# Two groups of four heads in one PSUM bank: one copy, sum broadcast, reciprocal, product and output projection for both

## The reference

```python
xn = _ln(x, ln1_w, ln1_b)
q, k, v = ((xn @ w + b).reshape(B, L, 16, 8) for w, b in ((q_w, q_b), (k_w, k_b), (v_w, v_b)))
scores = jnp.einsum('bqhd,bkhd->bhqk', q, k) * 8 ** (-0.5)
scores = jnp.where(causal, scores, -jnp.inf)
attn = jax.nn.softmax(scores, axis=-1)
attn_out = jnp.einsum('bhqk,bkhd->bqhd', attn, v).reshape(B, L, 128) @ o_w + o_b
...
x = x + alpha * attn_out + (1.0 - alpha) * ssm_out
```

## Time and profile before

| | |
|---|---|
| median of three runs | 1694.33 us |
| the profiled execution's own time | 1693.45 us |
| its span, first to last instruction | 1691.7 us |
| busy, TensorE products | 1443.8 us (85%) |
| busy, VectorE | 1292.0 us (76%) |
| busy, ScalarE | 1095.7 us (65%) |
| busy, GpSimd | 838.1 us (50%) |
| mean granted TensorE clock | 0.933 of full speed |

### The profile page before, as it was taken

How to read it: one execution, slowest core, us unless ns; L and a number is a source line. 1 busy time by engine, 2 the same in 40 slices (tenths; PEclk the granted TensorE clock), 3 DMA queues, 4 the chain that set the end, 5 groups by cost and what they waited for, 6 DMA issues and landing times. The chain is left out here.

```text
span 1691.7 us, 22138 instructions
## 1 busy us (share of the span) xinstructions
PE 1443.8 (85%) x7228; PEld 896.1 (53%) x7228; DVE 1292.0 (76%) x1945; ACT 1095.7 (65%) x1840; POOL 838.1 (50%) x867
## 2 busy tenths in 40 slices
PE   3678898888989898888867988899999999888787
PEld 3234544444444444444423735687786877635673
DVE  2149998989898999989924858688676777748857
ACT  2465667686767777686655756778878788621017
POOL 3136677768585867768743213022222222238843
PEclk9787899999999999999998999899999999958989
DMA  3112222222222222222002110011111111000001
GB/s 89 45 38 82 77 71 68 78 74 69 67 68 65 74 73 67 79 75 74 26 1 70 43 47 26 29 50 44 40 48 38 44 44 44 26 1 0 1 1 50
DMA packets 61656, 84.74 MB, mean 50 GB/s; under 512 B 6589, under 2 KB 32039, under 8 KB 61543
## 3 DMA queue, kind: packets, MB, share of 16 engines
q1 hardware_dynamic: 61442, 83.30, 16.3%
q10 hardware_dynamic: 100, 0.03, 0.0%
HBM read 74.38 MB, written 8.78 MB: 49 GB/s over the span
## 5 line engine op out<-in xcount | busy, mean ns | idle before, releaser
L1756 POOL TENSOR_TENSOR dBx<-dtx,Bb 128x512 f32<-128x512 f32 x256 | 319.4, 1270 | 10.9 <-DMA Bb<-b_dram 9.5
L1352 DVE TENSOR_TENSOR hl<-lsq,hh 128x512 fp32r<-128x512 f32 x320 | 262.6, 831 | 80.7 <-ACT hh L1641 72.4
L1322 DVE TENSOR_TENSOR_SCAN hy<-bank,dBx 128x512 f32<-128x512 f32 x256 | 297.9, 1203 | 19.1 <-ACT bank L1625 12.9
L1638 ACT ACTIVATE lsq<-bank,vcol 128x512 f32<-128x512 f32 x320 | 219.0, 692 | 105.5 <-DVE hl L1352 65.0
L1047 PE MATMUL bank<-QK 127*128 127x128 bf16 (+7 forms) x1024 | 234.4, 311 | 50.0 <-DVE Mx L1312 26.4
L1775 POOL TENSOR_TENSOR stage<-stage,lrs 128x512 f32<-128x512 f32 x64 | 90.5, 1414 | 312.2 <-DVE lrs L1432 312.2
L1312 DVE TENSOR_REDUCE Mx<-bank 128x1 f32<-128x384 f32 (+3 forms) x352 | 213.6, 627 | 41.1 <-PE bank L1047 40.0
L1047 PE MATMUL bank<-x,we1h 128*128 128x512 f32 x640 | 211.0, 412 | 18.0 <-ACT hh L1641 9.8
L1566 ACT ACTIVATE PT<-bank 128x512 f32<-128x512 f32 x320 | 184.5, 593 | 49.1 <-PE bank L1047 46.4
L1625 ACT ACTIVATE bank<-dtv,alog 128x512 f32<-128x512 f32 x256 | 170.5, 691 | 52.1 <-DVE hy L1322 51.3
L1258 DVE SCALAR_TENSOR_TENSOR hy<-bank,bc,hy 128x256 f32<-128x256 f32 x480 | 198.0, 473 | 3.9 <-PE bank L1174 3.1
(11 more groups left out here) (256 smaller groups left out, 2430.4 us busy)
## 6 DMA issues: line engine op xcount, KB each, us to landing
Bb<-b_dram SPq DMA_DIRECT2D x128, 256.0 KB, 3.6
stage<-w_rows SPq DMA_DIRECT2D x64, 256.0 KB, 3.3
parts<-part SPq DMA_DIRECT2D x16, 384.0 KB, 2.7
QK<-parts SPq DMA_DIRECT2D x64, 96.0 KB
QK<-parts SPq DMA_DIRECT2D x64, 64.0 KB
stage<-in_L_ffn_We_dram SPq DMA_DIRECT2D x16, 256.0 KB, 3.3
hy<-in_L_attn_x_dram SPq DMA_DIRECT2D x8, 256.0 KB, 5.4
QK<-parts SPq DMA_DIRECT2D x64, 32.0 KB
```

What stands on the lines that cost most here:

```text
L1322: engine.tensor_tensor_scan(hst[:, 2 * (g % 3) + h, :], bank[4 + h][:], dBx[:, g % 4, h, :], 0.0, ALU.mult, ALU.add).then_inc(sems["dve_sc ...
L1352: engine.tensor_tensor(hl[:, sl, :], full[:, f, :], hh[:, sl, :].bitcast(F32), ALU.subtract).then_inc(sems["dve_hl"], 1)
L1638: engine.activation(full[:, f, :], o[:], fn, bias=bias).then_inc(sems["act_up"], 1)
L1756: engine.tensor_tensor(dBx[:, sl, h], dtx[:, b % 2, h], Bb[:, sl], ALU.mult).then_inc(sems["pool_dbx"], 1)
```

## The change

Even and odd group now share bank 3. In `Vb` everything moves nine columns to the right, so that an even group's block of 32 columns begins with nine foreign columns and has its own head in rows 32i + 9 to 32i + 17 of the bank; the odd group follows with a block of nine columns only and overwrites rows 32i to 32i + 8 with its own head. It does not wait for a copy. After it one copy, one broadcast (row 32i + 8 onto rows 0 to 8, row 32i + 17 onto rows 9 to 17), one logarithm and exponential, one product and one product with an output weight that holds both groups' rows do the work of two. `normalise` is therefore begun for g = 1 and g = 3 only, `wo` follows it as before, `On` and `rdn` are indexed by the half batch, the output weights are loaded by eight DMAs in place of four (each half as large), `seld` is built by three selects in place of one, and the planner's cost of `wo` is halved. The cut diff:

```diff
-WORK = dict(..., pe_wo=190, ...
+WORK = dict(..., pe_wo=95, ...
...
     def weigh(b, g, units):
         k = 3
-        it = step("weigh", b=b, g=g, bank=k, free=free.get(f"b{k}"), ready=...,
+        it = step("weigh", b=b, g=g, bank=k, free=None if g % 2 else free.get(f"b{k}"), ready=...,
...
     def normalise(b, g, m):
-        gg, k = g % 2, 3
+        hf, k = g // 2, 3
...
-        it = step("on", ..., lrs_free=free.get(f"lrs{gg}"), on_free=free.get(f"On{gg}"))
+        it = step("on", ..., lrs_free=free.get(f"lrs{hf}"), on_free=free.get(f"On{hf}"))
...
-        it["o"] = free["Os"] = free[f"lrs{gg}"] = r_on[g] = up("pool_on")
+        it["o"] = free["Os"] = free[f"lrs{hf}"] = on = up("pool_on")
         for _ in range(4):
             yield
-        if gg == 0:
-            return
         k = take()
-        it = step("wo", ..., on=(r_on[g - 1], r_on[g]), h=h_last[b] or r_n[b])
-        it["m"] = free["On0"] = free["On1"] = up("pe_wo")
+        it = step("wo", ..., on=on, h=h_last[b] or r_n[b])
+        it["m"] = free[f"On{hf}"] = up("pe_wo")
...
-                later.append(normalise(b, g, m))
+                if g % 2:
+                    later.append(normalise(b, g, m))
...
-                        x = mm(o[32 * i:32 * i + 32, P * kj:T], Vb[:, b % 2, kj, 36 * g + 9 * i:36 * g + 9 * i + 32],
+                        c0, m = 36 * g + 9 * i + 9 * (g % 2), 9 if g % 2 else 32
+                        x = mm(o[32 * i:32 * i + m, P * kj:T], Vb[:, b % 2, kj, c0:c0 + m],
                                PT[:, sl, off:off + n], start=(kj == 0), stop=(kj == 3), pos=(0, 32 * i))
...
                 elif kind == "wo":
-                    q.wait_ge(("ld_wo", 64), it["on"], it["free"])
-                    mm(o[:], wo[:, it["g"] - 1, :], On[:, 0, :], start=True, stop=False)
-                    mm(o[:], wo[:, it["g"], :], On[:, 1, :], start=False, stop=True).then_inc(sems["pe_wo"], 1)
+                    q.wait_ge(("ld_wo", 128), it["on"], it["free"])
+                    mm(o[:], wo[:, it["g"] // 2, :], On[:, it["g"] // 2, :]).then_inc(sems["pe_wo"], 1)
...
-            engine.affine_select(out=sel, in_=sel, compare_op=ALU.not_equal, fill=1.0, base=-8, pattern=[[-32, 4], [0, 32]],
-                                 channel_multiplier=1).then_inc(sems["pool_set"], 1)
+            for c0, c1, row in ((0, 9, 8), (9, 18, 17), (18, 32, 8)):
+                engine.affine_select(out=sel[:, :, c0:c1], in_=sel[:, :, c0:c1], compare_op=ALU.not_equal, fill=1.0, base=-row,
+                                     pattern=[[-32, 4], [0, c1 - c0]], channel_multiplier=1).then_inc(sems["pool_set"], 1)
...
             for i in range(4):
-                engine.dma_start(wo[32 * i:32 * i + 8, :, :], d["L0_attn_o_w"].rearrange("(g i d) n -> i d g n", i=4, d=8)[i]).then_inc(sems["ld_wo"], 16)
+                for f, row in ((0, 9), (1, 0)):
+                    engine.dma_start(wo[32 * i + row:32 * i + row + 8, 0:2, :],
+                                     d["L0_attn_o_w"].rearrange("(a f i d) n -> i f d a n", a=2, f=2, i=4)[i][f]).then_inc(sems["ld_wo"], 16)
```

More of the change, by code:

```diff
@@ L167, in plan_mixers @@
     ring = [0, 1, 2, 6, 7]
-    r_parts, r_v, r_qk, r_mr, r_on = {}, {}, {}, {}, {}
+    r_parts, r_v, r_qk, r_mr = {}, {}, {}, {}
     h_last = [None] * NB
@@ L228, in weigh @@
         k = 3
-        it = step("weigh", b=b, g=g, bank=k, free=free.get(f"b{k}"), ready=(r_v[b], [(x, y) for _, _, x, y in units]),
+        it = step("weigh", b=b, g=g, bank=k, free=None if g % 2 else free.get(f"b{k}"), ready=(r_v[b], [(x, y) for _, _, x, y in units]),
                   blocks=sorted((kj, i, off, sl) for parts, sl, _, _ in units for i, kj, off in parts))
@@ L243, in normalise @@
         k = take()
-        it = step("on", b=b, g=g, o1=o1, bank=k, free=free.get(f"b{k}"), lrs_free=free.get(f"lrs{gg}"), on_free=free.get(f"On{gg}"))
+        it = step("on", b=b, g=g, o1=o1, bank=k, free=free.get(f"b{k}"), lrs_free=free.get(f"lrs{hf}"), on_free=free.get(f"On{hf}"))
         it["m"] = up("pe_dn")
@@ L998, in on_set @@
             return {name: i + 1 for i, name in enumerate(names.split())}
-        pool_set = on_set("vrow qk0 qk1 qk2 qk3 wo id0 id om cm on ep mask0 mask idb idn sel0 sel bsum vb0 mr vb qz0 qz1 qz2")
+        pool_set = on_set("vrow qk0 qk1 qk2 qk3 wo id0 id om cm on ep mask0 mask idb idn sel0 sel1 sel2 sel bsum vb0 mr vb qz0 qz1 qz2")
         dve_set = on_set("row0 row1 sc0 sc1 neg abs sgn2 max sgn gate om1 av2 av3 A qbs")
@@ L1557, in scalar_program @@
                 elif kind == "val":
-                    vv = Vb[:, it["b"] % 2, :, 0:144].rearrange("p t (h j) -> p t h j", j=9)[:, :, :, 0:8]
+                    vv = Vb[:, it["b"] % 2, :, 9:153].rearrange("p t (h j) -> p t h j", j=9)[:, :, :, 0:8]
                     q.wait_ge(("pool_set", pool_set["vb"]), it["m"], it["v_free"])
@@ L1570, in scalar_program @@
                 elif kind == "on":
-                    t = rdn[:, it["g"] % 2, :]
+                    t = rdn[:, it["g"] // 2, :]
                     q.wait_ge(it["m"], it["lrs_free"])
@@ L1719, in gpsimd_program @@
             q.wait_ge(("pool_set", pool_set["mr"]))
-            engine.memset(Vb[:, :, :, 0:144].rearrange("p a t (h j) -> p (a t) h j", j=9)[:, :, :, 8:9], 1.0).then_inc(sems["pool_set"], 1)
+            engine.memset(Vb[:, :, :, 9:153].rearrange("p a t (h j) -> p (a t) h j", j=9)[:, :, :, 8:9], 1.0).then_inc(sems["pool_set"], 1)
             for j in range(3):
@@ L1738, in gpsimd_program @@
                 elif kind == "on":
-                    gg = it["g"] % 2
+                    hf = it["g"] // 2
                     q.wait_ge(it["e2"], it["on_free"])
-                    engine.tensor_tensor(On[:, gg, :], Os[:], rdn[:, gg, :], ALU.mult).then_inc(sems["pool_on"], 1)
+                    engine.tensor_tensor(On[:, hf, :], Os[:], rdn[:, hf, :], ALU.mult).then_inc(sems["pool_on"], 1)
                 elif kind in ("wo", "so"):
```

4 lines of the change are left out of this document (2 added, 2 removed).

## The result

Four runs of the changed kernel: 1667.92, 1673.02, 1674.44 and 1675.11 us, median 1673.73. The kernel before took 1694.49 (1693.92 to 1700.46, four runs).

The account below looks back on a forecast made before the run. VectorE was taken to pace the mixer stage except 45 us per period where TensorE does; then the attention tail runs alone. 11.0 + 1.0 + 2.3 + 0.91 + 1.7 = 16.9 us off 1693.45: 1677 us, range 1668 to 1690.

Parts of the forecast that it names:

- The six stretches: Mixer stretches paced by TensorE: half the first projection and group 2's broadcast go, 1.83 us each time, 11.0 in all.
- only the projection's part survives the ScalarE work that follows: Lower bound for the mixer stretches paced by TensorE: 5.5 us in place of 11.0.
- ScalarE's relief counts too: Rival: ScalarE's removed work also pays, body 18.4 and tail 5.9 us, 1669 us in all; chance 0.14.
- The full stretches: Mixer stretches where VectorE is full: group 0's broadcast and half the second projection bring nothing.
- The tail: Last attention work, running alone after the mixer stage to 898 us: shorter by 5.9 us.
- Group 0: Last batch: its GpSimd product ahead of the gating product goes; 1.0 us, between 0 and 1.27.
- the two that stand on TensorE itself: Last batch, group 2: TensorE's wait for the copy, 1.33 us, and its broadcast, 0.96; taken as 2.3.
- 9 columns: Odd groups' stationary blocks, 9 columns instead of 32 at the same four positions: costs nothing.
- Not packed: Rival: 9-wide weighting blocks don't run beside the others, 135 us more, partly hidden; 1710 to 1810 us; chance 0.04.
- Setup: Start of the kernel: eight weight DMAs for four, three GpSimd selects for one; 0, at most 1.3 us slower.
- Slower by the clock: Rival: idler TensorE in VectorE-paced stretches gets 1.2 GHz more often, 0.9 us a dip; 40 dips give 1712; chance 0.05.
- a sign of being wrong: Granted TensorE clock falling below 0.97 from 140 to 857 us would show the forecast wrong.

Follow-up runs that it names:

- act_back: Changed kernel with three ScalarE activations per even group put back, on a tile nobody reads; 1679.10 us, ratio 0.9920 to the kernel before.
- pool_back: Changed kernel with one unread 128x512 GpSimd product per even group put back; 1676.52 us, ratio 0.9877 to the kernel before.
- wide: Changed kernel with the odd groups' stationary blocks 32 columns wide again; 1676.93 us, ratio 0.9910 to the kernel before.
- one_place: Changed kernel with weighting products of key blocks 1 to 3 all at the first head's array place and output rows; 1729.11 us, ratio 1.0227 to the kernel before.
- after_again: The changed kernel itself, timed and profiled once more; 1670.06 us, ratio 0.9862 to the kernel before.
- keep_tail: Changed kernel with eight unread TensorE products in three waits of the last batch; 1666.49 us, ratio 0.9818 to the kernel before.
- keep_band: Changed kernel with six unread projection products in TensorE's wait ahead of the band projections; 1667.00 us, ratio 0.9821 to the kernel before.

## Why the prediction was right, point by point

**The six stretches: 11.0 forecast, 11.2 measured, and that close by luck.** The period fell by 1.86 us and there are six. The step "I take 11.0, because the two waits of the earlier trace rows name TensorE" gave TensorE the whole 1.83. act_back, where TensorE is relieved and ScalarE is not, shows what that alone is worth: 0.91 us a period, 5.5 in all. That is the lower bound that the prediction gave this term, "only the projection's part survives the ScalarE work that follows". The projection gave its 0.87 (0.91 forecast). The broadcast of group 2 gave 0.03 us by itself, although the wait of 0.59 us behind it named TensorE and did vanish: VectorE waited longer for later products and as long for ScalarE's decay. The other half came with ScalarE. Its queue holds the silu block, with a table load ahead, between this place and the scan's decay; before and after:

```profile
540.50 1.28 ACT L1592 ACT_TABLE_LOAD   x1
```

```profile
528.61 1.28 ACT L1591 ACT_TABLE_LOAD   x1
```

Counted from the projection, the block starts at 22.54 us before (540.50 − 517.96), 20.68 after, 22.03 with TensorE's work back and 21.64 with ScalarE's. These are the gains of the period, 1.86, 0.51 and 0.90, to a hundredth: ScalarE's queue set the pace to the scan, and both engines fed it. The rival *ScalarE's relief counts too* had that mechanism, at a price of 1.23 us a stretch on top of TensorE's 1.83; measured are 0.51 a period with TensorE's work back and 0.95 with it gone. A missing half and an unforecast one came to the same sum.

**The full stretches: nothing, as forecast.** In the undisturbed period the lead of after is 8.17 us at its first projection (424.12 against 415.95) and 10.02 at this scan, before and after:

```profile
453.12 2.34 DVE L1322 TENSOR_TENSOR_SCAN hy<-bank,dBx 128x512 f32<-128x512 f32 x2 [1.00 <-ACT bank L1625]
```

```profile
443.10 2.34 DVE L1321 TENSOR_TENSOR_SCAN hy<-bank,dBx 128x512 f32<-128x512 f32 x2 [0.60 <-ACT bank L1624]
```

At the next projection it is 10.03 (517.96 against 507.93). All of the 1.86 is gained before the scan; the broadcast of group 0 and the second projection, which lie behind it, bring 0.01.

**The tail: 5.9 forecast, 5.37 measured.** Group 0: from the last accumulation to `zg,wso` 5.11 before (861.27 − 856.16) and 4.12 after: 0.99, forecast 1.0. From first to last projection 16.04 and 12.71: 3.33, forecast 2.3 + 0.91 = 3.2. From the last projection to the next stage 5.80 and 4.04: 1.76, forecast 1.7. Against these, from `zg,wso` to the first projection 15.30 and 16.01: 0.71 lost, since `zg,wso` ran at the lower clock for longer, 3.78 for 3.04. The terms were right in size to about a tenth, and what was left out is the clock.

Their reasons were not all right. With GpSimd's product back the first distance stays 4.12, with ScalarE's work back it is 4.70: the product that stood there in the kernel before had waited 1.19 us for ScalarE's exponential, and the one that pool_back gives back waits for nothing. The second distance is 13.57 with TensorE's products back (from the zero product that stands ahead of the first projection), 14.26 with ScalarE's and 13.23 with GpSimd's. TensorE's 0.86 us match the projection and leave nothing for the broadcast; of the 2.3 us for group 2, "the two that stand on TensorE itself", 1.55 come back with ScalarE's work and 0.52 with GpSimd's. The last distance is 5.78 with TensorE's products back and so TensorE's alone.

**9 columns: nothing**, right by the rows of wide and one_place; the time of wide does not show it, since it stood 3 to 7 us above the change for a reason that stayed open. *Not packed* did not happen; its factor was four, and losing the packing measured 3.4.

**Setup.** Eight DMAs in the queue:

```profile
16.22 2.70 SPq L1813 DMA_DIRECT2D wo<-in_L_attn_o_w_dram  x8
```

2.70 us where it was 1.34, as forecast. The first product of the norms (`hT,cmat`) starts at 36.08, before at 35.52; in the other kernels with eight DMAs it starts between 35.45 and 36.74, so the 0.56 us lies within the scatter of the setup.

**Slower by the clock** did not decide, but its mechanism is there in both kernels. In the body of before, five periods from 233.97 to 707.24 took 473.27 us, where five of 93.84 are 469.2. The broadcast that stood in one of them:

```profile
392.61 1.98 PE L1047 MATMUL bank<-Os,seld 128*128 128x512 f32 x2
```

It took 1.98 us where that of the earlier trace rows took 1.08. After lost nothing to this in its five periods (459.88 = 5 × 91.98), and after_again 1.4 us. The prediction also named a sign of being wrong, a granted clock below 0.97 between 140 and 857 us. It is 0.98 in after but 0.96 in after_again and 0.95 in wide, and the period held: at this size the sign did not tell. So of the 16.5 us by which after ends its accumulations earlier, 11.2 are the change, about 4.1 are the clock of the one profile of before, and the rest lies ahead of 234 us (2.0 gained) and behind 707 (0.7 lost). The same holds for the whole: what the rows show of the change, 11.2 + 5.4, is 16.6 us, near the 16.9 forecast, and the medians differ by 20.8 and, in the set of after_again, by 24.0. These 4 to 7 us no experiment placed. Whether before's executions meet more such dips than the changed kernel's as a rule stays open, since there is one profile of it.

## What to carry to other kernels

If an engine that is not the pacing one holds up the pacing engine in one stretch per period, take the length of that wait (0.98, 0.59) as a bound on the relief and not as its price; then look for the next wait behind it (here 1.00 us for ScalarE) and see whether the same change moves that too. Where it did not, the 0.59 was worth 0.03; where it did, the reliefs of both engines together were worth 0.98. To find out, give each engine its work back by itself and read the distance between two marks, not only the total. Stacking two groups in one bank through narrower stationary blocks halves all that follows the bank and costs TensorE nothing, as long as the blocks stay at different places of the array. And where TensorE must wait a few microseconds ahead of a dense stretch, a few unread products in the wait can be worth nearly half as much as such a change: 0.6% here, beside the change's own 1.3%. In one of three profiles with the wait ahead of the band filled, the clock fell all the same.

## What the runs showed of the hardware

In some executions a busy TensorE did not get its clock back for a long time. Busy us by stretch, after and then after_again:

```profile
1465.00:1485.00 20.00, 20.00 (x29) 7.29 (x29) 8.04 (x6) 5.08 (x19) 10.45 (x5) 0.50 0.00 0
```

```profile
1465.00:1485.00 20.00, 17.16 (x43) 6.65 (x42) 10.46 (x8) 7.73 (x28) 12.91 (x5) 0.98 0.00 0
```

The same program, the same wait of 5.77 us ahead of it. In after the products run at 1.2 GHz although TensorE is busy 20.00 of 20 us, and the band lasts 33.98 us; in after_again the third projection is back at 2.4 GHz, and the band lasts 27.83. Eight of the fourteen profiles in the table show the long form. Between these two profiles the band differs by 6.15 us. The executions of the change range from 1667.92 to 1675.11; that the band makes most of this is likely but not shown, since only two of them were profiled. The Trainium skill, TensorE: Matmul & The Clock Gate, section What's actually happening, has it that activity releases the throttled state. The band of after_again, with its third projection back at 0.91 us, agrees; the 20 us at 0.50 above do not: activity did not release it there. keep_tail and keep_band show another thing, that with work in the wait ahead the clock had mostly not fallen at all. Why, no run here shows.
